# Eight-expert layer in a GNN and transformer kernel: the last expert's tile moved to the end, its output spread by one-hot products, and the next tile's scaling cut in three

## Chip, cores and metric

The kernel runs on one core of one Trainium2 chip. The metric is the device time of one execution in microseconds. Times of this program are shown as the median of its runs; the trace comes from one further execution under the profiler.

## The reference, cut to what matters

The program first runs a two-layer graph convolution and a 12-head causal attention over 625 tokens of 768 values. The change concerns what comes after: each token goes to one of eight experts, by the largest of eight gate values, and the output of that expert is added to the token.

```python
h2 = _ln(x, ln2_g, ln2_b).reshape(-1, d)
gate_logits = h2 @ Wg                       # 625 x 8
w, sel = jax.lax.top_k(gate_logits, K)      # K = 1
w = jax.nn.softmax(w)
combine = zeros.at[arange(n)[:, None], sel].add(w)
hid = relu(einsum('nd,edf->enf', h2, W1) + b1[:, None, :])   # W1: 8 x 768 x 3072
y = einsum('enf,efd->end', hid, W2) + b2[:, None, :]         # W2: 8 x 3072 x 768
return x + einsum('ne,end->nd', combine, y)
```

## The kernel before

**Engines and order.** One core; each engine has its own program, written by hand in its block (SP issues the weight loads, POOL the others, ACT, DVE and PE compute), and they meet through semaphores. Nothing is reordered: an engine does what stands next, and waits if it must.

**Tokens to tiles.** The 625 tokens stand in five groups of 125 (`C = 5`, `P = 125`). DVE works out for every token its expert, its rank in it and a row number `slot` (L1088 to L1154). A tile is 128 rows (`CAP`) of one expert. An expert with more than 128 tokens would get further tiles at the end of the list; `over[0]` is their number `n_over`. POOL scatters the normalised tokens `n2` to the DRAM tensor `hs_d` by `slot` (L515), and gathers the bias rows of `b2` into `x2` (L520). Tile 0 doesn't wait for the scatter: PE picks its tokens with one-hot matrices `oh0` (L1552).

**A tile** (function `tile` on each engine). The expert's weights are 18.9 MB of float32 in 16 chunks, 8 of W1 and 8 of W2, each 128 x 2304 (1152 KB). A chunk is loaded to one of four buffers `raw` (L417, L420), copied by ACT to a rounded `whi` (L557, from `split_hi`), and DVE writes the rest, raw minus whi, to `wlo` (L825, from `split_lo`). There are four `whi`/`wlo` pairs. A `raw` buffer is free for the chunk four later when its `wlo` is written. PE makes three products for each pair of operands (hi x hi, hi x lo, lo x hi): 18 matmuls of 384 columns for a chunk. In step k of a tile ACT does `split_hi` of chunk k+3 and then reads out PE's result of chunk k-1 to `hid` (L792); DVE does `split_lo` of chunk k+2. For W1, PE turns `hid` around (L1566), DVE adds the bias (L1179), ACT and DVE split it to `hTTh` and `hTTl` (L557, L823). The W2 products (L1593) collect in PSUM banks 4 and 5 and are copied to `ysb` by ACT and DVE at the start of the next tile (L785, L1175), and stored by POOL to `ys_d` (L530).

**The next tile's tokens.** POOL loads them to `hs` (L527). After W2 chunk 1, PE turns them to PSUM banks 6 and 7 (L1544). ACT scales them in six pieces to `hgf` (L767) and rounds them to `hgh` (L557), all in step `k == FCH + 2` (`FCH = 8`), after the `split_hi` of that step. DVE writes `hgl` in the same step (L1158, recorded at L825), and only then goes on to the `split_lo` of the next step.

**End.** Tiles 1 to 7 run in a loop (`Fori(1, E)`). Then comes a loop of four turns (`K_OVER`) over the further tiles, each skipped by an `If` when `s >= n_over` (PE: L1605 to L1608); in this execution all four were skipped on every engine. Then `ysb` is filled for the last time (L812, L1211), stored (L541), and POOL gathers each token's row of `ys_d` to `x2` in five indirect DMAs (L545). DVE adds `x2` times the gate weight to `base` (L1214), and SP stores the five parts of the output (L435).

## Time and profile before

| | us |
|---|---|
| three runs | 962.91, 964.02, 969.46 (median 964.02) |
| profiled execution, its own time | 963.17 |
| span of the profiled execution | 961.6 |
| mean granted TensorE clock | 0.968 of full speed |
| busy: PE, PEld, DVE, ACT, POOL | 867.0, 835.7, 709.2, 545.3, 90.9 |

PE is the matmul array, PEld its weight loads. Times in the profile count from the start of the span; the device time is 1.6 us longer than the span. The expert tiles fill the stretch from about 474 us to 937 us; what follows is the end described above.

### The profile page before, as it was taken

How to read it: one execution, taken by the hardware profiler on the slowest of the kernel's cores; microseconds unless marked ns; L12 is line 12 of the kernel's file. 1: busy time of each engine (PE TensorE's matmuls, PEld its weight loads, DVE VectorE, ACT ScalarE, POOL GpSimd, SP SyncE). 2: the span in 40 equal slices, each digit the busy share in tenths (PEclk: the TensorE clock that was granted, in tenths of full speed). 3: DMA queues.
4: the chain of work that ended last, by engine and by line, in shares of the span. 5: the costliest groups of instructions: out<-in, count | busy, mean ns of one | idle time of the engine just before them, and what ended most of it. 6: DMA issues, size and time to landing. Idle time of an engine off the chain costs nothing.

```text
span 961.6 us, 14800 instructions
## 1 busy us (share of the span) xinstructions
PE 867.0 (90%) x5410; PEld 835.7 (87%) x5410; DVE 709.2 (74%) x1076; ACT 545.3 (57%) x753; POOL 90.9 (9%) x92
## 2 busy tenths in 40 slices
PE   7999898989997888898878899999999999999990
PEld 7999898989996667798868899999999999899990
DVE  7996265773327999744666998898979889897962
ACT  4503232352226787624447587787868788686850
POOL 2000014220003100021630000000000000000002
PEclk9999799999999998999898999999999999999995
DMA  7020008255217500230698999999999999999935
GB/s 220 10 91 1 2 1 150 69 154 101 99 50 212 197 1 1 82 99 1 219 268 322 306 354 340 371 327 381 347 350 332 342 373 331 380 337 353 350 130 177
DMA packets 117094, 197.88 MB, mean 206 GB/s; under 512 B 34599, under 2 KB 83967, under 8 KB 117046
## 3 DMA queue, kind: packets, MB, share of 16 engines
q1 hardware_dynamic: 107796, 169.08, 53.2%
q0 software_dynamic: 7424, 26.09, 8.4%
q10 hardware_dynamic: 1826, 2.06, 0.8%
q8 instruction: 32, 0.52, 0.2%
q14 instruction: 16, 0.13, 0.0%
HBM read 179.29 MB, written 17.90 MB: 205 GB/s over the span
## 4 chain that ended last, share of the span: by engine, by line
PE 51%; DVE 19%; DMA 14%; issue 7%; ACT 7%; POOL 2%; SPq 0%; DVEq 0%; ACTq 0%; POOLq 0%
PE ps L1579 13%; PE ps L1236 11%; DMA raw<-in_L_ffn_W 11%; PE ps L1593 7%; PE ps L1412 7%; DVE wlo L825 6%; PE ps L1265 4%; PE ps L1566 2%; PE ps L1472 2%; DVE pTl L825 2%; ACT whi L557 2%; ACT hgf L767 2%; DVE pr L1025 1%; DMA hs_d<-n,slot 1%; DVE pr L1032 1%
## 5 line engine op out<-in xcount | busy, mean ns | idle before, releaser
L825 DVE TENSOR_TENSOR wlo<-raw,whi 128x2304 fp32r<-128x2304 f32 x137 | 349.9, 2570 | 20.3 <-ACT whi L557 20.1
L557 ACT ACTIVATE whi<-raw 128x2304 fp32r<-128x2304 f32 x139 | 295.3, 2130 | 107.1 <-DMA raw<-in_L_ffn_W 66.1
L1579 PE MATMUL ps<-whi,hgh 128*128 128x384 f32 x384 | 135.1, 352 | 3.9 <-DVE hgl L825 2.8
L1593 PE MATMUL ps<-whi,hTTh 128*128 128x384 f32 x384 | 131.7, 343 | 0.0
L1579 PE MATMUL ps<-whi,hgl 128*128 128x384 f32 x384 | 130.8, 341 | 0.0
L1579 PE MATMUL ps<-wlo,hgh 128*128 128x384 f32 x384 | 130.0, 339 | 0.0
L1593 PE MATMUL ps<-wlo,hTTh 128*128 128x384 f32 x384 | 129.8, 338 | 0.0
L1593 PE MATMUL ps<-whi,hTTl 128*128 128x384 f32 x384 | 129.6, 338 | 0.0
L1579 PEld LDWEIGHTS ps<-whi,hgh 128*128 128x128 f32 x384 | 73.6, 192 | 4.3 <-DVE hgl L825 2.9
L1579 PEld LDWEIGHTS ps<-wlo,hgh 128*128 128x128 f32 x384 | 73.8, 192 | 0.0
L1579 PEld LDWEIGHTS ps<-whi,hgl 128*128 128x128 f32 x384 | 73.2, 191 | 0.0
L1593 PEld LDWEIGHTS ps<-wlo,hTTh 128*128 128x128 f32 x384 | 72.2, 188 | 0.0
L1593 PEld LDWEIGHTS ps<-whi,hTTh 128*128 128x128 f32 x384 | 72.1, 188 | 0.0
L1593 PEld LDWEIGHTS ps<-whi,hTTl 128*128 128x128 f32 x384 | 72.1, 188 | 0.0
L1265 PE MATMUL ps<-ohd,ohs 125*125 125x314 bf16 x400 | 58.9, 307 | 7.5 <-DVE ohd L877 5.8
L1265 PEld LDWEIGHTS ps<-ohd,ohs 125*125 125x125 bf16 x400 | 54.9, 142 | 10.3 <-DVE ohd L877 8.3
L1566 PE MATMUL ps<-ident,hid 128*128 128x128 f32 x192 | 32.6, 278 | 23.5 <-ACT hid L792 23.5
L1566 PEld LDWEIGHTS ps<-ident,hid 128*128 128x128 f32 x192 | 23.8, 142 | 30.2 <-ACT hid L792 28.6
L823 DVE SCALAR_TENSOR_TENSOR hTTl<-bia,hTTh 128x384 fp32r<-128x384 f32 x64 | 35.4, 553 | 19.4 <-ACT hTTh L557 19.4
L1179 DVE TENSOR_TENSOR bia<-ps,b1T 128x384 f32<-128x384 f32 x64 | 35.6, 556 | 15.5 <-PE ps L1566 15.5
L557 ACT ACTIVATE qh<-ps 64x125 fp32r<-64x125 f32 (+1 forms) x66 | 20.4, 309 | 44.9 <-PE ps L1412 23.0
L1449 PE MATMUL ps<-ident,pr 125*125 125x125 f32 x168 | 32.1, 307 | 10.9 <-DVE pr L1032 7.7
(264 smaller groups left out, 1744.6 us busy)
## 6 DMA issues: line engine op xcount, KB each, us to landing
raw<-in_L_ffn_W SPq DMA_DIRECT2D x128, 1152.0 KB, 7.0
hs_d<-bc POOLq DMA_DIRECT2D x13, 384.0 KB, 6.4
raw<-in_L_gnn_W SPq DMA_DIRECT2D x4, 1152.0 KB, 5.6
ys_d<-ysb POOLq DMA_DIRECT2D x9, 384.0 KB, 5.9
hs<-hs_d POOLq DMA_DIRECT2D x8, 384.0 KB, 5.5
raw<-in_L_ffn_Wv SPq DMA_DIRECT2D x6, 384.0 KB, 5.2
raw<-in_L_ffn_Wq SPq DMA_DIRECT2D x6, 384.0 KB, 5.2
raw<-in_L_ffn_Wk SPq DMA_DIRECT2D x6, 384.0 KB, 5.3
```

The lines of the kernel that those rows point to most:

```text
L557: act.activation(out_, in_, func).then_inc(s, 1)
L767: act.activation(hgf[:, m, :], blocks(6, 128, DC, CAP)[:, m, :], ACT.Identity, scale=lnT[:, 2 * DC + m:2 * DC + m + 1], bias=lnT[:, 3 * DC ...
L823: dve.scalar_tensor_tensor(out_, in_, 0.0, hi_, ALU.max, ALU.subtract).then_inc(s, 1)
L825: dve.tensor_tensor(out_, in_, hi_, ALU.subtract).then_inc(s, 1)
L1179: dve.tensor_tensor(bia[:, k % 2, :, :], blocks(2 + k % 2, 128, JW, CAP), bcol.rearrange("p (j o) -> p j o", o=1).broadcast_to((128, JW, C ...
L1236: ins = mm(ps[0:P, bank + half, 0:HB], l, rr, start=m == 0 and i == 0, stop=m == DC - 1 and i == 2)
L1265: ins = mm(ps[0:P, m, 0:HALF], ohs[:, i % EU, m * P:(m + 1) * P], ohd[:, i % EU, :], start=i in BOUNDS, stop=i + 1 in BOUNDS)
L1412: ins = mm(ps[:, 2 * (m % 2) + half, 0:HALF], l, rr, start=c == 0 and i == 0, stop=c == DC - 1 and i == 2)
L1449: ins = nc.tensor.transpose(turned_part(u)[:, b, :], pr[:, u % PRS, b * P:(b + 1) * P], ident[0:P, 0:P])
L1566: ins = nc.tensor.transpose(blocks(2 + k % 2, 128, JW, CAP)[:, j, :], hid[0:CAP, k % 2, j * 128:(j + 1) * 128], ident[0:CAP, 0:CAP])
L1579: ins = mm(ps[0:CAP, k % 2, 0:FW], l, rr, start=m == 0 and j == 0, stop=m == DC - 1 and j == 2)
L1593: ins = mm(ps[0:CAP, 4 + half, 0:HB], l, rr, start=k == 0 and j == 0 and jj == 0, stop=k == FCH - 1 and j == JW - 1 and jj == 2)
```

## The change

**Order of the tiles.** The loop runs tiles 0 to 6, then come the further tiles (if any), then expert 7 as the last tile, written out once more on every engine. The row numbers are shifted to suit: further tiles start at number 7 and expert 7's rows go behind them.

**The last tile's output** no longer goes through DRAM. DVE marks each token that belongs to it in `oh0` again (five operations, during tile 0), PE turns these marks in the place where the other tiles turn the next tile's tokens, and ACT copies them to `ohl`. At the end ACT and DVE split the last tile's output to hi and lo in two halves, PE multiplies each token group's marks with them (four matmuls for a group), and DVE adds the product, read from PSUM, to `base`. POOL stores the output of the tile before, and gathers the five groups' rows from `ys_d`, while the last tile runs; DVE adds these to `base` after its last `split_lo`. The output is stored from `base`.

**Scaling of the next tile.** ACT's six pieces are done two at a time in the steps FCH+2, FCH+3 and FCH+4, each after the `split_hi` of its step; DVE's `hgl` moves to step FCH+5, behind its last `split_lo`.

```diff
+LAST_BANK = (0, 2, 6, 4, 0)
+TILE_STEPS = {FCH + 2: (0, 1), FCH + 3: (2, 3), FCH + 4: (4, 5)}
...
+                     ("ohl", [128, C, P], F32R)])
@@ SP
-            with sp.Fori(1, E) as t:
+            with sp.Fori(1, E - 1) as t:
                 weights(t, t)
...
-                    weights(e, s + E)
+                    weights(e, s + E - 1)
+            weights(E - 1, n_over + E - 1)
             for c in range(C):
                 sp.wait_ge(s_fin, c + 1)
                 for r0, r1 in PARTS:
-                    sp.dma_start(tok(out)[r0:r1, c, :], x2[r0:r1, c, :]).then_inc(s_out, 16)
+                    sp.dma_start(tok(out)[r0:r1, c, :], base[r0:r1, c, :]).then_inc(s_out, 16)
@@ POOL
-            for t in range(E + 1, TILES + 1):
+            for t in range(E, TILES + 1):
                 g.dma_start(ys_d[t * CAP:(t + 1) * CAP, :], bc[0][0:CAP, :]).then_inc(s_zero, 16)
...
-            with g.Fori(0, E) as t:
+            with g.Fori(0, E - 1) as t:
                 tile(t)
...
-            g.wait_ge(s_yev, 2 * (n_over + E) + 2)
-            g.dma_start(ys_d[bass.ds((n_over + E) * CAP, CAP), :], ysb[0:CAP, :]).then_inc(s_ylast, 16)
+            g.wait_ge(s_yev, 2 * (n_over + E - 1) + 2)
+            g.dma_start(ys_d[bass.ds((n_over + E - 1) * CAP, CAP), :], ysb[0:CAP, :]).then_inc(s_ylast, 16)
@@ ACT
-                    if k == FCH + 2:
-                        tile_in(t + 2, DC * t + 2 * DC)
+                    if last:
+                        if k == FCH + 2:
+                            a.wait_ge(s_ohT, 1)
+                            hi(ohl[:, :, :], blocks(6, 128, C, P), s_ohl)
+                        continue
+                    if k in TILE_STEPS:
+                        tile_part(t + 2, TILE_STEPS[k])
+                    if k == max(TILE_STEPS):
+                        tile_hi(DC * t + 2 * DC)
...
-            act.activation(ysb[0:CAP, 0:HB], ps[0:CAP, 4, 0:HB], ACT.Copy).then_inc(s_yev, 1)
+            tile(n_over + E - 1, last=True)
+            for half in range(2):
+                a.wait_ge(s_yhalf, half + 1)
+                hi(hg[0][:, 3 * half:3 * half + 3, :], blocks(4 + half, 128, 3, CAP), s_yh)
@@ DVE
-            step(dve.tensor_tensor(own, own, kk, ALU.add))
-            dve.tensor_copy(slot[:, :], own).then_inc(s_slot, 1)
+            step(dve.tensor_tensor(kk, kk, late, ALU.add))
+            step(dve.tensor_tensor(home, own, kk, ALU.add))
+            dve.tensor_copy(slot[:, :], home).then_inc(s_slot, 1)
...
             tile_in(1)
+            for c in range(C):
+                dve.tensor_scalar(oh0[:, c, :], iotac[:, :], float(CAP * (E - 1)), own[:, c:c + 1],
+                                  ALU.add, ALU.is_equal).then_inc(s_ohe, 1)
             split_lo(3, 0)
...
-                    if k == FCH + 2:
+                    if k == max(TILE_STEPS) + 1 and not last:
                         tile_in(t + 2)
...
+            tile(E - 1, n_over + E - 1, last=True)
+            d.wait_ge(s_base2, C)
             for c in range(C):
                 d.wait_ge(s_yg[c], 16)
-                dve.scalar_tensor_tensor(x2[:, c, :], x2[:, c, :], wtok[:, c:c + 1], base[:, c, :],
+                dve.scalar_tensor_tensor(base[:, c, :], x2[:, c, :], wtok[:, c:c + 1], base[:, c, :],
+                                         ALU.mult, ALU.add).then_inc(s_yin, 1)
+            for half in range(2):
+                d.wait_ge(s_yh, half + 1)
+                part = slice(3 * half, 3 * half + 3)
+                lo(hg[1][:, part, :], blocks(4 + half, 128, 3, CAP), hg[0][:, part, :], s_yl)
+            d.wait_ge(s_yin, C)
+            for c in range(C):
+                d.wait_ge(s_sel, c + 1)
+                bv = base[:, c, :].rearrange("p (a b) -> p a b", a=2)
+                dve.scalar_tensor_tensor(bv, wide(LAST_BANK[c], P), wtok[:, c:c + 1], bv,
                                          ALU.mult, ALU.add).then_inc(s_fin, 1)
@@ PE
-            with pe.Fori(1, E) as t:
+            with pe.Fori(1, E - 1) as t:
                 tile(t)
             pe.wait_ge(s_route, 1)
             n_over = pe.value_load(over[0:1, 0:1], min_val=0, max_val=K_OVER)
             with pe.Fori(0, K_OVER) as s:
                 with pe.If(s < n_over):
-                    tile(s + E)
+                    tile(s + E - 1)
+            tile(n_over + E - 1, last=True)
+            pe.wait_ge(s_ohl, 1)
+            def spread_y(c, half):
+                for i, t in enumerate(hg):
+                    ins = mm(ps[0:P, LAST_BANK[c] + half, 0:HB], ohl[:, c, :],
+                             t[:, 3 * half:3 * half + 3, :].rearrange("p a b -> p (a b)"), start=i == 0, stop=i == 1)
+                return ins
+            pe.wait_ge(s_yl, 1)
+            for c in range(C - 1):
+                spread_y(c, 0)
+            pe.wait_ge(s_yl, 2)
+            for c in range(C - 1):
+                spread_y(c, 1).then_inc(s_sel, 1)
+            pe.wait_ge(s_fin, 1)
+            spread_y(C - 1, 0)
+            spread_y(C - 1, 1).then_inc(s_sel, 1)
```

What stands on ACT in steps FCH+2 to FCH+4 of tile 0 before (names in brackets are semaphores; chunks_used is counted by PE, tile_turned says that the next tile's tokens are in PSUM):

```order
L557 ACTIVATE whi<-raw 128x2304 [waits raw_in1,chunks_used]
L767 ACTIVATE hgf<-ps,lnT 128x128 [waits tile_turned]
L767 ACTIVATE hgf<-ps,lnT 128x128 x5
L557 ACTIVATE hgh<-hgf 128x768 [waits tile_scaled]
L557 ACTIVATE whi<-raw 128x2304 [waits raw_in2,chunks_used]
L557 ACTIVATE whi<-raw 128x2304 [waits raw_in3,chunks_used]
```

and in the changed kernel, whose lines here are numbered eight higher:

```order
L565 ACTIVATE whi<-raw 128x2304 [waits raw_in1,chunks_used]
L775 ACTIVATE hgf<-ps,lnT 128x128 [waits tile_turned]
L775 ACTIVATE hgf<-ps,lnT 128x128
L565 ACTIVATE whi<-raw 128x2304 [waits raw_in2,chunks_used]
L775 ACTIVATE hgf<-ps,lnT 128x128 [waits tile_turned]
L775 ACTIVATE hgf<-ps,lnT 128x128
L565 ACTIVATE whi<-raw 128x2304 [waits raw_in3,chunks_used]
L775 ACTIVATE hgf<-ps,lnT 128x128 [waits tile_turned]
L775 ACTIVATE hgf<-ps,lnT 128x128
L565 ACTIVATE hgh<-hgf 128x768 [waits tile_scaled]
```

Two weight copies have moved ahead of four of the scaling pieces and of the rounding.

On DVE, the end of the program before:

```order
L825 TENSOR_TENSOR wlo<-raw,whi 128x2304
L1207 UNCONDITIONAL_BRANCH
L1205 REGISTER_ALU
L1205 COMPARE_AND_BRANCH
L1209 ISA
L1211 COPY ysb<-ps 128x384
L1214 SCALAR_TENSOR_TENSOR x<-x,wtok,base 125x768 x5
```

and in the changed kernel:

```order
L844 TENSOR_TENSOR wlo<-raw,whi 128x2304
L1241 SCALAR_TENSOR_TENSOR base<-x,wtok,base 125x768 x5
L844 TENSOR_TENSOR hgl<-ps,hgh 128x384 x2
L1251 SCALAR_TENSOR_TENSOR base<-ps,wtok,base 125x768 x5
```

The branches of the further tiles now stand ahead of the last tile instead of behind it, and five more additions follow the last weight chunk.

## Rows read from the trace of the kernel before

**Rows 1.** The chain that ended last: start us, us, what (x count)

```profile
515.90 3.17 PE ps L1593 x18
...
574.70 3.17 PE ps L1593 x18
...
720.95 4.69 PE ps L1579 x18
...
854.70 3.17 PE ps L1593 x18
...
893.46 3.15 PE ps L1579 x18
896.61 0.33 PE ps L1566 x3
...
910.84 3.17 PE ps L1593 x18
...
917.49 0.65 PE ps L1544 x6
918.15 19.02 PE ps L1593 x108
```

**Rows 2.** Timeline of ACT: start us, us, line, operation [idle before <-releaser]

```profile
863.43 2.19 ACT L767 ACTIVATE hgf<-ps,lnT 128x128 f32<-128x128 f32 x6
...
876.20 2.13 ACT L557 ACTIVATE whi<-raw 128x2304 fp32r<-128x2304 f32 x1 [2.43 <-DMA raw<-in_L_ffn_W]
```

**Rows 3.** Timeline of DVE, the same stretch

```profile
866.53 0.96 DVE L825 TENSOR_TENSOR hgl<-hgf,hgh 128x768 fp32r<-128x768 f32 x1 [2.23 <-ACT hgh L557]
867.41 9.96 DVE L825 TENSOR_TENSOR wlo<-raw,whi 128x2304 fp32r<-128x2304 f32 x4
```

**Rows 4.** Timeline of PE, the stretch just after

```profile
888.81 0.55 PE L1566 MATMUL ps<-ident,hid 128*128 128x128 f32 x3 [1.53 <-ACT hid L792]
```

**Rows 5.** Stretches: length, busy of PE PEld DVE ACT POOL, clock, DMA share, GB/s

```profile
845.00:861.00 16.00, 16.00 (x97) 15.87 (x97) 16.00 (x14) 13.30 (x14) 0.00 (x0) 1.00 0.98 341
...
869.00:873.00 4.00, 4.00 (x25) 4.00 (x24) 4.00 (x3) 2.92 (x2) 0.00 (x0) 1.00 0.66 208
...
873.00:887.00 14.00, 14.00 (x82) 13.96 (x80) 11.73 (x6) 8.29 (x6) 0.54 (x1) 1.00 1.06 375
```

**Rows 6.** The end: chain that ended last

```profile
937.19 0.57 DVE ysb L1211
...
938.43 3.98 DMA ys_d<-ysb
...
948.82 7.47 DMA x<-ys_d,slot
...
956.31 1.02 DVE x L1214
```

**Rows 7.** One line's operations (ns min/median/max): the branches on PE, loads on DVE

```profile
L1602 PEldq COMPARE_BRANCH  x7: 76/208/220, 597.8 to 933.9; - x7
...
L1606 PEldq COMPARE_BRANCH  x4: 83/221/252, 938.7 to 941.7; - x4
...
L1607 PEldq COMPARE_BRANCH  x4: 221/224/3625, 934.9 to 941.3; - x4
...
L1206 DVEq TENSOR_LOAD <-over x4: 297/314/330, 928.0 to 931.6; - x4
```

**Rows 8.** Stretches behind the last matmul (columns as in rows 5)

```profile
937.00:940.00 3.00, 0.15 (x1) 0.00 (x0) 0.56 (x1) 0.49 (x1) 0.54 (x1) 1.00 0.18 67
940.00:961.00 21.00, 0.00 (x0) 0.00 (x0) 5.09 (x5) 0.00 (x0) 6.09 (x5) 0.50 0.60 193
```

**Rows 9.** Gathers beside weight loads in tile 0: a stretch

```profile
484.00:504.00 20.00, 13.02 (x77) 12.31 (x76) 12.25 (x13) 9.05 (x10) 4.84 (x5) 0.98 1.04 258
```

**Rows 10.** The chain that ended last, in the same part

```profile
492.20 15.75 DMA raw<-in_L_ffn_W
```

**Rows 11.** Timeline of DVE before the scatter

```profile
462.52 0.17 DVE L1143 TENSOR_TENSOR rt<-rt 125x5 f32<-125x5 f32 x1
```

More of the change, by code:

```diff
@@ L212, in build @@
         rt, tp, iotac, oh0 = R1["rt"], R1["tp"], R1["iotac"], R1["oh0"]
+        ohl = R3["ohl"]
         hTT = (R3["hTTh"], R3["hTTl"])
@@ L316, in build @@
         s_yg = [sem(f"y_back{c}") for c in range(C)]
+        s_ohe, s_ohT, s_ohl, s_yhalf, s_yh, s_yl, s_sel, s_yin = (sem(n) for n in (
+            "last_expert_marked", "marks_turned", "marks_ready", "last_y_half", "last_y_hi", "last_y_lo", "last_y_spread",
+            "other_y_added"))
         s_yev, s_yst, s_ylast, s_zt, s_fin, s_out = (sem(n) for n in (
@@ L761, in _, with tile_part @@
             split_hi(2, 0)
-            def tile_in(n_in, n_a):
+            def tile_part(n_in, part):
                 a.wait_ge(s_hgT, n_in)
-                for m in range(DC):
+                for m in part:
                     act.activation(hgf[:, m, :], blocks(6, 128, DC, CAP)[:, m, :], ACT.Identity,
@@ L769, in tile_in, with tile_hi, tile @@
                                    bias=lnT[:, 3 * DC + m:3 * DC + m + 1]).then_inc(s_hga, 1)
+            def tile_hi(n_a):
                 a.wait_ge(s_hga, n_a)
                 hi(hg[0][:, :, :], hgf[:, :, :], s_hgh)
-            tile_in(1, DC)
+            tile_part(1, range(DC))
+            tile_hi(DC)
             split_hi(3, 0)
-            def tile(t, first):
+            def tile(t, first=False, last=False):
                 for k in range(SCH):
@@ L798, in tile @@
                         hi(hTT[0][:, JW * (k - 2):JW * (k - 1), :], bia[:, k % 2, :, :], s_hTh2, ACT.Relu)
-                    if k == FCH + 2:
-                        tile_in(t + 2, DC * t + 2 * DC)
-            tile(0, True)
-            with a.Fori(1, E) as t:
-                tile(t, False)
+                    if last:
[7 more added lines that the diff above has]
+                        tile_hi(DC * t + 2 * DC)
+            tile(0, first=True)
+            with a.Fori(1, E - 1) as t:
+                tile(t)
             a.wait_ge(s_route, 1)
@@ L1117, in _ @@
             kk = rt[:, 6, 16:16 + C]
+            late = rt[:, 6, 24:24 + C]
+            home = rt[:, 9, 0:C]
             tk = rt[:, 8, 0:E * K_OVER].rearrange("p (e k) -> p e k", k=K_OVER)
@@ L1162, in _, with tile @@
             tile_in(1)
+            for c in range(C):
+                dve.tensor_scalar(oh0[:, c, :], iotac[:, :], float(CAP * (E - 1)), own[:, c:c + 1],
+                                  ALU.add, ALU.is_equal).then_inc(s_ohe, 1)
             split_lo(3, 0)
-            def tile(e, t, first):
+            def tile(e, t, first=False, last=False):
                 for k in range(SCH):
@@ L1189, in tile @@
                            hTT[0][:, JW * (k - 2):JW * (k - 1), :], s_hTl2, relu=True)
-                    if k == FCH + 2:
+                    if k == max(TILE_STEPS) + 1 and not last:
                         tile_in(t + 2)
-            tile(0, 0, True)
+            tile(0, 0, first=True)
             d.wait_ge(s_base, C)
@@ L1199, in _ @@
                                          ALU.mult, ALU.add).then_inc(s_base2, 1)
-            with d.Fori(1, E) as t:
-                tile(t, t, False)
+            with d.Fori(1, E - 1) as t:
+                tile(t, t)
             d.wait_ge(s_route, 1)
@@ L1555, in _, with tile @@
             keep_busy(TURN_BUSY, onesb[:, :], onesb[:, :], 3)
-            def tile(t):
-                first = isinstance(t, int)
+            def tile(t, first=False, last=False):
                 pe.wait_ge(s_hgl, t + 1)
@@ L1594, in tile @@
                                          stop=k == FCH - 1 and j == JW - 1 and jj == 2)
-                    ins.then_inc(s_used, 1)
+                        if last and k == FCH - 1:
+                            ins.then_inc(s_yhalf, 1)
+                    if not last or k < FCH - 1:
+                        ins.then_inc(s_used, 1)
                     if k == 0:
                         turn_hid(FCH - 1)
-                    if k == 1:
+                    if k == 1 and last:
+                        pe.wait_ge(s_ohe, C)
+                        for c in range(C):
+                            ins = nc.tensor.transpose(blocks(6, 128, C, P)[:, c, :], oh0[:, c, :], ident[0:P, 0:P])
+                        ins.then_inc(s_ohT, 1)
+                    elif k == 1:
                         tile_in(s_hs, 16 * t + 16, t + 1)
-            tile(0)
-            with pe.Fori(1, E) as t:
+            tile(0, first=True)
+            with pe.Fori(1, E - 1) as t:
                 tile(t)
```

26 lines of the change are left out of this document (12 added, 14 removed).

## The prediction

> **What bounds the kernel now.** I read the chain that ended last first. It shows the same picture tile after tile from 574 us on: PE carries it, chunk by chunk, and hands it to ACT, DVE and a weight load only around the passage from one tile to the next. That chain gives a floor for a tile [rows 1]: W1 is 8 chunks of 3.15 us with 7 turnings of 0.33 us between them (27.5), W2 is two chunks of 3.17, the last turning of 0.33, the 0.65 of the next tile's tokens and 19.02 for the other six chunks (26.35), together 53.85 us. The starts of W2 lie 280.0 us apart over five tiles (574.70 to 854.70), so the passages 1-2 to 5-6 cost 280.0 - 5 x 53.85 = 10.75 us above the floor, 2.15 each. Passage 6-7 costs 56.14 - 53.85 = 2.3, passage 0-1 58.80 - 53.85 = 4.95.
>
> Second, the timelines of ACT, DVE and PE at one passage tell why. ACT does the six scalings in one piece from 863.43 to about 865.7 and the rounding behind them, and only then the next weight copy [rows 2]. DVE stands still 2.23 us for that, writes hgl in 0.96, and has then four chunks to split in one go [rows 3]. As a raw buffer comes free only when its wlo is written, the load that could have been issued at about 864.3 + 2.55 = 866.9 is issued at 867.41 + 2.5 = 870.0. The DMA queues run partly dry for it (208 GB/s from 869 to 873) and are then full at 375 GB/s without catching up [rows 5]. ACT waits 2.43 us for a load at 876.20 [rows 2], and some chunks later PE waits 1.53 us for the hid that ACT has behind such a copy [rows 4]. Once the stall was so long that the clock fell: 18 matmuls took 4.69 instead of 3.15 us at 720.95 [rows 1].
>
> Third, the end. From the end of the last matmul at 937.19 to the end of the span at 961.6 PE has no part in it: 24.4 us of read-out, store, five gathers and five additions [rows 6].
>
> **The end, new.** Let the last matmul end at 0. The first half of the output (9 of 18 matmuls, 0.175 us each from 3.15 / 18) is complete 1.6 us earlier, and its split on ACT and DVE, two operations like the read-out of 0.57 [rows 6], is hidden by the second half. From 0: PE spreads the first half for four groups, 8 x 0.175 = 1.4; beside it the second half is split, 2 x 0.57 = 1.15. The second half of group 0 is two matmuls, 0.35, with a handover of some 0.2 it is there at 1.95. Then DVE sets the pace, five additions of 1.02 [rows 6] (these had one operand less in PSUM; I take the same), to 7.05. The fifth group waits for a bank but needs only 0.7 of PE. The output store behind the last addition takes what it takes now, 961.6 - 957.33 = 4.27. Sum 11.3 instead of 24.4: **-13.1 us**. If the five stores, now 1.02 apart, queue up, it is a microsecond less; range -12 to -13.6.
>
> The five additions of gathered rows (5.1 us) lie behind DVE's last weight split, where DVE has nothing to do until the last tile ends; hidden unless the gathers are over 10 us late.
>
> **The passages.** With the scaling in three, each weight copy comes at its own time; the two scalings, about 0.73 us, fit in the time in which ACT waits for PE to release a buffer. DVE no longer waits, so the loads are issued 1.7 to 3.1 us earlier. The copies that waited for loads then wait for PE, as in the middle of a tile. hgl comes some 7 us later than now but still about 7 us ahead of the next tile's first matmul. Whether the queues can deliver is close: 18.9 + 0.4 + 0.4 = 19.7 MB for a tile at 375 GB/s are 52.5 us, against a floor of 53.85. So the stall can go, with hardly any reserve. I take five sixths of the 10.75: **-9.0**, range 0 to -10.75; a gain on the other side of the floor is excluded, and a loss of 1 us a tile (hgl's 0.96 before the next wlo) is the unlikely other end. At 0-1, DVE's five additions to base stand between the tiles and stay there, so I take **-1.5** of 4.95 (0 to -4). Passage 6-7 is counted next.
>
> **The further tiles' loop in mid-stream.** All engines now pass the four skipped turns between tiles 6 and 7, where they did it at the end, when only POOL mattered. On PE the sequencer left the tile loop at 933.9, while the array had work to 937.19, and its last branch began at 941.7 [rows 7]. One branch, the first skip, took 3.63 us; the others 0.22. So the array stands idle from 937.2 to 941.8, and with the tile's own waits some 4.9 us. In the last rows the clock was full up to 940 and half after it, some 3 us behind the last matmul [rows 8]; I take that it falls here too and costs what it cost once, 4.69 - 3.15 = 1.5 [rows 1]. The 2.3 of the old passage go. Net 4.9 + 1.5 - 2.3 = **+4.1**, range 0 to +8. DVE's loads of the skipped turns are 1.2 us apart (928.0 to 931.6) [rows 7], about 6 us in all, and SP has a like loop before it issues expert 7's first load; both begin before PE's does and are hidden by PE's gap. If PE's gap were not there, they would cost some 3 us instead.
>
> **The gathers beside the last tile.** Five times 384 KB is 1.92 MB, at 375 GB/s 5.1 us of DMA time that tile 7 has not spent till now. They are issued in its W1 part, where the queues moved 341 of 375 GB/s [rows 5], a reserve of 9% or 2.5 us in 27.5; the idle gap before also lets the loads get ahead. From below the cost is 0. The nearest row from above is tile 0: there scatter and gathers ran beside the loads, the total fell to 258 GB/s, PE was busy for 13.0 of 20 us [rows 9], and one load took 15.75 us [rows 10]. That is 7 us for more than twice these bytes. I take **+2**, range 0 to +7.
>
> **Small ones.** The slots need two more DVE steps in a chain of 0.17 us ones [rows 11], 0.35 on the way to the scatter. The five new marks fall in a place where DVE waits for ACT; 0 to 1. Together **+0.4**. The zeroed tile more is far ahead under the attention, and copying the turned marks replaces ACT's scaling in the last tile: nothing.
>
> **Sum**, against the profiled execution's own 963.17: -13.1 - 9.0 - 1.5 + 4.1 + 2.0 + 0.4 = -17.1, so 946.1. That execution lies 0.85 below the median of 964.02, so I predict **947**.
>
> **The rivals.**
> A. The weight loads are the true bound, and the passages stay as they are: they only wait for data at another place. For it: 375 GB/s without a break from 873 to 887, and 52.5 against 53.85. Against it: 208 GB/s just before, and 341 in mid-tile. Then 9.0 + 1.5 are missing: 957.5. 10%.
> B. The gathers hurt as in tile 0, 7 instead of 2: 952. For it rows 9 and 10; against it, tile 0 carried the scatter too, and its gather of bias rows reads only eight different rows. 10%.
> C. The loop costs PE next to nothing, because its first skip took 3.63 us only with the array running empty. Then 947 less about 5: 942. 8%.
> D. Slower. The eight far branches on PE (four skips, four turns) each fetch their target, and in mid-stream they do it against weight loads. At 3.63 each that is 29 us instead of the 5.2 of rows 7, giving 971; at one and a half times that, since loads more than doubled their time in tile 0, 43.5 and 985. It decides from about 26 us on top of the forecast, that is, branches of 3.9 us. For it: one skip did cost 3.63. Against it: the same skip cost 0.22 three times more, and the tile loop's own branch, as far, cost 0.2 seven times [rows 7]. 4%.
>
> The Trainium skill (Runtime: NRT & Kernel Launch, section Instruction fetch mechanics) says that a taken branch whose target is outside the current window of two pages has to fetch the page by DMA before the engine goes on. By that rule all far branches here pay, which is rival D; the trace bears it out for one branch of the eight and for none of the loop's.
>
> **How the numbers follow.** The forecast has 68%; its own range, from the terms above, is 940 to 953. A measurement of this kernel tells about 1% (9.6 us) from no change. Faster by more, that is below 954.4: nearly all of the forecast, B mostly, C, and a little of A: 84%. Within 1%: most of A, the edges of the others: 13%. Slower: most of D, 3%. The range 939 to 957 leaves out D, half of A and something at the lower end.
>
> **What would show it.** In the new profile: the last matmul of W2 to the end about 11 us with PE, DVE and the stores in it and no POOL; distances between starts of W2 of 54 to 54.5 instead of 56.0 for tiles 1 to 6; no wait of hgl for ACT and no dip at the passage; a hole of about 5 us in PE before tile 7 and half clock after it; small waits of ACT for weight loads in tile 7 behind the gathers. It is wrong if the distances stay at 56 (A), if the hole is far from 5 us (C, D), or if tile 7's W1 takes over 31 us (B).

## The result, and the profile after

The changed kernel takes 959.45 us (median of 13 runs, 954.62 to 963.68); the kernel before took 964.24 in the same session (13 runs). The ratio is 0.9941, with a 95% interval of 0.9918 to 0.9964: half a per cent faster, 5 us where 17 were forecast, and above the range of 939 to 957. The profiled execution took 956.24 us with a span of 954.7, mean granted clock 0.967; it lies 3.2 us below the median of the changed kernel's runs. So the miss is 12.5 us in the median (959.45 against 947) and 10.2 us in the profile, whose terms the table compares.

A table of the starts of W2 of each tile (the first matmuls of L1593 before, L1630 after) shows where the time went. The rows that begin a passage or a tile in the chain that ended last give the same numbers.

| us, one profiled execution each | before | after | difference | forecast |
|---|---|---|---|---|
| up to tile 0's W2 | 515.90 | 517.44 | +1.5 | +0.4 |
| tile 0 to tile 1 | 58.80 | 57.38 | -1.4 | -1.5 |
| tile 1 to tile 6, five distances | 280.00 | 269.99 | -10.0 | -9.0 |
| tile 6's W2 to the last matmul of tile 7 | 82.49 | 98.10 | +15.6 | +6.1 (4.1 and 2.0) |
| last matmul to the end of the span | 24.4 | 11.8 | -12.6 | -13.1 |
| span | 961.6 | 954.7 | -6.9 | -17.1 |

Four of the five lines came within 1.1 us. Nearly the whole miss of the profile is in one: the last 98 us of PE's work, 9.5 us over the forecast.

**What went as forecast.** The chain that ended last, of the kernel after (start us, us, what), a steady tile and then the end:

```profile
690.72 19.00 PE ps L1630 x108
709.72 6.26 PE ps L1616 x36
...
942.91 1.81 PE ps L1660 x10
...
944.81 2.87 DVE base L1251 x3
```

At 709.72, 36 matmuls of the next tile's W1 follow the last of W2 without any step on another engine between them; [rows 1] and [rows 4] had the hand-over there. The five distances are 54.0 us on average, against a floor of 53.85. Behind the last matmul stand 1.81 us of PE, the additions and the store.

ACT in the same passage (timeline: idle before and releaser in brackets):

```profile
693.99 2.14 ACT L565 ACTIVATE whi<-raw 128x2304 fp32r<-128x2304 f32 x1 [1.06 <-PE ps L1630]
696.03 0.79 ACT L775 ACTIVATE hgf<-ps,lnT 128x128 f32<-128x128 f32 x2
697.09 2.14 ACT L565 ACTIVATE whi<-raw 128x2304 fp32r<-128x2304 f32 x1 [0.26 <-PE ps L1630]
```

Two scalings (0.79 us) fit between two weight copies, and ACT still waits for PE afterwards; in [rows 2] six of them stood ahead of a copy. The stretches of that passage (length, busy of PE PEld DVE ACT POOL, clock, DMA share, GB/s), the first two 15 and 19 us behind tile 3's start of W2, as in [rows 5] behind tile 6's, and the third in W1 of tile 7:

```profile
698.00:702.00 4.00, 4.00 (x25) 4.00 (x24) 3.46 (x3) 3.97 (x5) 0.00 (x0) 1.00 1.07 376
702.00:716.00 14.00, 14.00 (x82) 13.97 (x82) 11.29 (x6) 10.11 (x7) 0.54 (x1) 1.00 1.07 376
...
886.00:906.00 20.00, 18.05 (x107) 16.99 (x105) 16.95 (x14) 11.67 (x12) 7.57 (x3) 1.00 0.99 265
```

The dent of 208 GB/s in [rows 5] is gone: 376 GB/s from the first microsecond on. That settles rival A, which wanted the loads to be the bound; they run at full rate and keep up, with next to no reserve.

**What did not.** The third row is tile 7's W1 beside the gathers. The queues are in use for 0.99 of the time and move 265 GB/s, where they moved 344 in the second half of tile 7's W1 before (896 to 911 us) and 341 in tile 6's [rows 5]:

```profile
896.00:911.00 15.00, 15.00 (x93) 14.84 (x92) 15.00 (x15) 12.50 (x14) 0.00 (x0) 1.00 0.99 344
```

PE's timeline of the kernel after, the operations that stood waiting between tile 6's last matmul and tile 7's W2:

```profile
878.10 0.68 PE L1616 MATMUL ps<-whi,hgh 128*128 128x384 f32 x1 [6.98 <-issue]
...
897.29 0.55 PE L1603 MATMUL ps<-ident,hid 128*128 128x128 f32 x3 [0.63 <-ACT hid L803]
...
902.07 0.55 PE L1603 MATMUL ps<-ident,hid 128*128 128x128 f32 x3 [1.08 <-ACT hid L803]
...
910.15 0.90 PE L1603 MATMUL ps<-ident,hid 128*128 128x128 f32 x3 [4.39 <-ACT hid L803]
```

and from the chain that ended last:

```profile
878.10 8.13 PE ps L1616 x36
...
893.13 14.39 DMA raw<-in_L_ffn_W
...
911.05 5.37 PE ps L1616 x18
```

Against the floor of 80.2 us (53.85, and 26.35 for the last W2) the 98.1 contain 17.9. They are nearly all in these rows: 6.98 of hole, 1.83 for the time at half clock behind it (8.13 instead of 2 x 3.15; the granted clock was 0.50 from 878 to 880 us), 6.10 of waits for hid, behind a weight load that took 14.39 us, and 2.79 for the two groups after the longest wait (5.37 instead of 3.15, 0.90 instead of 0.33, at a granted clock of 0.50 from 911 to 915 us). Sum 17.7. The hole and its clock are 8.8 where the prediction had 6.4, and the gathers' part 8.9 where it had 2.0. "<-issue" at the first row means that no other engine was waited for: PE's own sequencer, the part that takes the branches, was late. Its branches (PEldq; ns, min/median/max), and DVE's first split behind its own four skipped turns:

```profile
L1652 PEldq COMPARE_BRANCH  x4: 221/224/5524, 868.9 to 877.3; - x4
```

```profile
868.25 5.03 DVE L844 TENSOR_TENSOR wlo<-raw,whi 128x2304 fp32r<-128x2304 f32 x2 [4.16 <-issue]
```

Again one skip of four pays, now 5.52 us (3.63 in [rows 7]), and three cost 0.22. All six kernels below and here that keep the skips on PE in this place show it, with 5.46 to 5.92 us. Beside full queues (378 GB/s from 868 to 870 us) a transfer of 16 KB on an instruction queue, taken here for the page behind the branch, began 3.1 us after it; in the kernel before, with no loads under way, 1.0 us after it.

### The profile page after: what moved, and what is told of

Its sections match the earlier page's. It is cut to its first block, busy times and chain, and to the rows that moved or that the text cites. A ratio compares the mean times of both kernels' runs of the same rounds, so it can differ in the third digit from the quotient of the medians.

```text
span 954.7 us, 14785 instructions
## 1 busy us (share of the span) xinstructions
PE 874.0 (92%) x5429; PEld 843.1 (88%) x5429; DVE 714.1 (75%) x1089; ACT 544.7 (57%) x748; POOL 95.1 (10%) x91
## 4 chain that ended last, share of the span: by engine, by line
PE 63%; DVE 18%; DMA 7%; issue 5%; ACT 4%; POOL 1%; DVEq 1%; SPq 0%; ACTq 0%; POOLq 0%
PE ps L1630 16%; PE ps L1616 14%; PE ps L1273 12%; PE ps L1449 7%; DMA raw<-in_L_ffn_W 5%; DVE wlo L844 5%; PE ps L1302 4%; DVE pTl L844 2%; PE ps L1509 2%; PE ps L1603 2%; DVE pr L1044 2%; DMA hs_d<-n,slot 2%; DVE pr L1051 1%; ACT whi L565 1%; POOL hs_d L523 1%
## 5 line engine op out<-in xcount | busy, mean ns | idle before, releaser
L1630 PE MATMUL ps<-whi,hTTh 128*128 128x384 f32 x384 | 131.6, 343 | 0.0
L1630 PE MATMUL ps<-wlo,hTTh 128*128 128x384 f32 x384 | 129.8, 338 | 0.0
L1630 PE MATMUL ps<-whi,hTTl 128*128 128x384 f32 x384 | 129.7, 338 | 0.0
L1630 PEld LDWEIGHTS ps<-wlo,hTTh 128*128 128x128 f32 x384 | 72.2, 188 | 0.0
L1630 PEld LDWEIGHTS ps<-whi,hTTh 128*128 128x128 f32 x384 | 72.2, 188 | 0.0
L1630 PEld LDWEIGHTS ps<-whi,hTTl 128*128 128x128 f32 x384 | 72.1, 188 | 0.0
```

The lines of the kernel that those rows point to most:

```text
L1630: ins = mm(ps[0:CAP, 4 + half, 0:HB], l, rr, start=k == 0 and j == 0 and jj == 0, stop=k == FCH - 1 and j == JW - 1 and jj == 2)
```

## Experiments

Ten kernels were run. All times are medians, and each ratio is against runs of the kernel before that were made beside it; their median was 964.79 us for e1 to e4, 966.36 for e5 to e8 and 963.79 for e9 and e10, so kernels of different groups are compared by their ratios. The distances come from one profiled execution of each kernel, and how far they vary from one execution to the next was not measured. The traces of e4_three_only and e8_one_loop_split are of the slowest execution of each (959.52 and 947.11 us), in which tile 0's W2 began only at 525.5 and 523.9. The texts written ahead of the runs give the hole before tile 7 as 7.5 us; between PE's weight loads the trace shows 7.30, between matmuls, as above, 6.98. First all distances in one table; "tile 6 to 7" is from start of W2 to start of W2, "tail" from the last matmul of W2 to the end of the span.

| kernel | us | ratio (95%) | five distances | tile 6 to 7 | tail |
|---|---|---|---|---|---|
| before | 964.24 | 1 | 280.0 | 56.1 | 24.4 |
| after | 959.45 | 0.9941 (0.9918 to 0.9964) | 270.0 | 71.9 | 11.8 |
| e1_gate | 955.19 | 0.9898 (0.9861 to 0.9934) | 270.9 | 63.5 | 17.5 |
| e2_pe_plain | 957.10 | 0.9932 (0.9906 to 0.9958) | 271.0 | 69.9 | 11.9 |
| e3_rows_direct | 954.94 | 0.9906 (0.9874 to 0.9938) | 270.3 | 67.8 | 11.8 |
| e4_three_only | 952.92 | 0.9864 (0.9824 to 0.9904) | 269.6 | 54.2 | 24.1 |
| e5_last_alone | 967.78 | 1.0017 (0.9997 to 1.0038) | 281.5 | 69.0 | 11.8 |
| e6_no_skips | 950.14 | 0.9834 (0.9796 to 0.9873) | 269.6 | 66.1 | 11.9 |
| e7_later_split | 949.77 | 0.9827 (0.9788 to 0.9866) | 270.0 | 63.6 | 13.7 |
| e8_one_loop_split | 939.95 | 0.9701 (0.9670 to 0.9731) | 269.3 | 55.3 | 13.5 |
| e9_dve_plain | 956.76 | 0.9936 (0.9903 to 0.9970) | 269.4 | 68.5 | 12.1 |
| e10_three_adds_ahead | 940.47 | 0.9752 (0.9689 to 0.9815) | 270.5 | 55.6 | 12.6 |

### The two halves of the change apart

**e4_three_only**: the kernel before, with only its scaling cut in three.

```diff
-                    if k == FCH + 2:
-                        tile_in(t + 2, DC * t + 2 * DC)
+                    if k in TILE_STEPS:
+                        tile_part(t + 2, TILE_STEPS[k])
+                    if k == max(TILE_STEPS):
+                        tile_hi(DC * t + 2 * DC)
@@ DVE
-                    if k == FCH + 2:
+                    if k == max(TILE_STEPS) + 1:
```

> The kernel before with the scaling of the next tile in three steps and hgl at step FCH+5, nothing else of the change. Theory (this alone gave the passages' 10.0 + 1.4 us, and passage 6-7 gives its 2.3 too): distances between starts of W2 of about 53.9 us, span 947.5 to 949, time 949 to 951, faster than the whole change. Rival (the passages improved because the order of the tiles or the code changed): distances stay at 56, span 959 to 962.

Measured: 952.92 us, 1.9 over the expected range, 1.4% faster than before, and its interval lies below that of the whole change. Six distances from tile 1 to tile 7 are 53.75 to 54.27, as the theory said.

**e5_last_alone**: the change with the scaling in one step again.

```diff
-TILE_STEPS = {FCH + 2: (0, 1), FCH + 3: (2, 3), FCH + 4: (4, 5)}
+TILE_STEPS = {FCH + 2: (0, 1, 2, 3, 4, 5)}
@@ DVE
-                    if k == max(TILE_STEPS) + 1 and not last:
+                    if k == FCH + 2 and not last:
```

> The change without its other half: the last expert is run last and spread by products, but the next tile is scaled in one step at FCH + 2 again, on ACT and DVE. Theory (the two halves add up, and moving the last expert costs about as much before tile 7 as it saves behind it: 15.6 against 12.6 us): the five distances come back to 280 us in all, 10 us over those of the change, and the time is 966 to 971 us, not faster than before and likely 2 to 6 us slower. Rival (the last expert moved is a gain of some us by itself, and only hidden by the tighter schedule of the three parts, which leaves the loads no slack for the gathers): the distance from tile 6's to tile 7's start is under 68 us here, and the time 958 to 963 us.

Measured: 967.78 us, ratio 1.0017 with 1 in the interval. The five distances are back at 281.5, the tail stays at 11.8, tile 6 to 7 at 69.0. Moving the last expert alone is no gain: 12.6 us saved at the end, 12.9 (69.0 - 56.1) given back ahead of it. The theory expected 2 to 6 us slower and got 1.4; the two halves do not quite add up, since 0.9864 x 1.0017 = 0.988 and the whole change has 0.994. The missing 0.006 is 5.8 us, against some 0.005 of uncertainty from the three intervals, and the distances show where most of it would lie: with the scaling in three the move costs 71.9 - 54.2 = 17.7 us ahead of tile 7 instead of 12.9. Of these 4.8 us, 1.9 are no cost of the move: passage 6-7 still had its own stall before (56.1 against 54.2), and behind the hole that stall no longer counts. The other 2.9 (71.9 against 69.0) would be the rival's part, that the tighter schedule leaves the loads less slack for the gathers; one execution of each shows it. The whole gain of the change, and more, comes from the scaling in three (0.9864 alone, 0.9941 with the last expert moved).

### What the last tile pays for: the gathers

**e1_gate**: the five gathers wait until ACT has copied the turned marks, some 10 us into W2 of tile 7.

```diff
             g.wait_ge(s_base2, C)
+            g.wait_ge(s_ohl, 1)
```

> The changed kernel, but POOL's five gathers wait for the copied marks (ohl), which ACT writes right after its copy of weight chunk 13 of the last tile, when only the last two loads are under way. Theory (the gathers take the DMA engines from the weight loads of the last tile's W1; that cost 9.2 us of waits and half clock there): the waits of 1.1, 1.6 and 4.9 us in W1 of the last tile go, the distance from the start of W2 of tile 6 to that of tile 7 falls from 71.9 to about 63 us, the hole of 7.5 us before tile 7 stays, the gathers end some 22 us into a W2 of 26 and delay nothing: span about 945.5 us, time 947. Rival (the waits come from the loads that SP and DVE issued late behind the skipped turns, and from the half clock after the hole): W1 of the last tile still waits as long, span 953 to 956.

Measured: tile 6 to 7 in 63.5 us as against 71.9, and W1 of tile 7 without a wait. The 8.4 us that this takes away are the gathers' part. But the tail grew to 17.5, since the gathers came too late, and so the time of 955.19 is 8 us over the expected 947. DVE and PE at the end of this kernel (timelines):

```profile
938.62 1.02 DVE L1242 SCALAR_TENSOR_TENSOR base<-x,wtok,base 125x768 f32<-125x768 f32 x1 [1.37 <-DMA x<-ys_d,slot]
939.55 1.02 DVE L845 TENSOR_TENSOR hgl<-ps,hgh 128x384 fp32r<-128x384 f32 x2
```

```profile
940.25 0.65 PE L1661 MATMUL ps<-hgh,ohl 128*125 128x384 f32 x1 [4.28 <-DVE hgl L845]
```

The split of y, the last tile's output (hgl), stands behind the fifth gathered addition on DVE, and PE waits 4.28 us for it. That is queueing, not bandwidth: the additions are needed only at the very end.

**e3_rows_direct**: the same bytes, but each gather replaced by a plain load of 125 rows in a row, so that tokens do not get their own rows of y.

```diff
-                g.indirect_dma_start(out=x2[:, c, :], out_offset=None, in_=ys_d[:, :],
-                                     in_offset=bass.IndirectOffsetOnAxis(ap=slot1[:, c:c + 1], axis=0)
-                                     ).then_inc(s_yg[c], 16)
+                g.dma_start(x2[:, c, :], ys_d[CAP + c * P:CAP + (c + 1) * P, :]).then_inc(s_yg[c], 16)
```

> The changed kernel with the five indirect gathers replaced by five plain loads of the same size, 125 rows standing next to each other, issued by POOL at the same place; the tokens' rows are not picked, so that part of the computation is left out. Theory (the indirect gather is poor traffic: the queues moved 264 GB/s beside it instead of 375, and it costs the weight loads 11 us of DMA time for 5.1 us worth of bytes): with plain loads the total stays near 375 GB/s, the waits in W1 of the last tile fall from about 7 to 1 to 3 us, span 947 to 950. Rival (any 1.92 MB at that place cost as much): waits as before, span 953 to 956.

Measured: 954.94 us with a span of 952.7, so between the theory's span (947 to 950) and the rival's (953 to 956); tile 6 to 7 in 67.8 us, 4.1 less than after, and still 4.3 more than in e1_gate. The stretch of W1 that answers to after's 265 GB/s, and its two parts:

```profile
886.00:906.00 20.00, 18.09 (x101) 17.67 (x100) 13.38 (x12) 14.18 (x14) 0.79 (x2) 0.93 1.03 320
...
888.00:898.00 10.00, 10.00 (x62) 9.90 (x61) 7.77 (x8) 7.17 (x8) 0.00 (x0) 1.00 1.04 263
898.00:906.00 8.00, 6.09 (x31) 5.76 (x30) 5.61 (x5) 5.84 (x6) 0.00 (x0) 0.85 1.00 378
```

So about half of the gathers' 8.4 us stays when the same bytes come as plain loads, and half goes. The rate doesn't tell the two forms apart: 263 GB/s with plain loads under way, 265 with gathers. What differs is how long they are under way. The plain loads' packets fill the 10 us from 888 to 898, and behind them the queues are back at 378 GB/s; the gathers' packets are spread over all 20 us from 886 to 906. POOL issued the five plain loads within 2.7 us and the five gathers within 11.3. Whether the longer time comes from the gathers' form or from their slower issue, no run separates.

**e7_later_split**: gathers released by the turning of the marks on PE, and two gathered additions (`add_y`, with `EARLY = 2`) ahead of the split of y, three behind it.

```diff
+            g.wait_ge(s_ohT, 1)
@@ DVE
+            for c in range(EARLY):
+                add_y(c)
...
-            d.wait_ge(s_yin, C)
-            for c in range(C):
+            for c in range(C):
+                if c >= EARLY:
+                    add_y(c)
+                d.wait_ge(s_yin, c + 1)
                 d.wait_ge(s_sel, c + 1)
```

> The change with its gathers released by the marks' turning on PE (about 7 us into W2 of tile 7) and DVE's gathered additions split: two ahead of the split of y, three behind it, each just ahead of its token block's last addition. The skipped turns stay. Theory (the gathers cost by running beside the last loads, and cost nothing behind them if no split of y is queued behind them): distance to tile 7 63 to 64 us as with the wait for the marks, tail 12 to 13.5 us instead of 17.5, time 950 us (948 to 952). Rival (gathers 4 us earlier collide with the last load, or the row-wise transfers are simply too slow for the 20 us that are left): PE waits 2 us or more in the last passes of W2, or the tail stays over 15 us, and the time is 953 or more.

Measured: 949.77 us, tile 6 to 7 in 63.6, tail 13.7, no wait of PE in W2. The first gather began 8.2 us behind the start of W2, against 10.4 in e1_gate, so only 2.2 us earlier and not 4. The rest is as the theory said, the tail 0.2 over its range; the 2 us of tail over after's 11.8 are the three additions now on the path (3.0 us), less 1.3 by which the stores, now further apart, end sooner behind the last one (3.9 instead of 5.2).

### What the last tile pays for: the skipped turns

**e2_pe_plain**: the four skipped turns taken out on PE only, so that PE could run no further tile; **e9_dve_plain**: out on DVE only; **e6_no_skips**: out on all engines. For PE:

```diff
-            pe.wait_ge(s_route, 1)
-            n_over = pe.value_load(over[0:1, 0:1], min_val=0, max_val=K_OVER)
-            with pe.Fori(0, K_OVER) as s:
-                with pe.If(s < n_over):
-                    tile(s + E - 1)
-            tile(n_over + E - 1, last=True)
+            tile(E - 1, last=True)
```

> The changed kernel with the four skipped turns left out on PE alone; what PE thereby leaves out is the tiles of an expert with more than 128 tokens, of which this input has none. Theory (the hole is PE's first skip, 5.5 us, plus the other branches): the hole before tile 7 falls from 7.5 to under 1 us and the half clock after it goes, together 9 us less; the loads of the last tile then have less lead, so the gathers' waits grow by up to 4: span 945.5 to 950. Rival (DVE's own skipped turns, 5.9 us, keep chunk 0's wlo away and hold PE as long): the hole stays over 4 us, span 951 or more.

Measured: 957.10, a clear miss of what was expected (945.5 to 950). The hole of 7 us went, and the waits in W1 of tile 7 took its place:

```profile
881.27 0.55 PE L1603 MATMUL ps<-ident,hid 128*128 128x128 f32 x3 [2.92 <-ACT hid L803]
...
900.45 0.73 PE L1603 MATMUL ps<-ident,hid 128*128 128x128 f32 x3 [4.45 <-ACT hid L803]
...
914.77 0.47 PE L1603 MATMUL ps<-ident,hid 128*128 128x128 f32 x1 [5.59 <-ACT hid L803]
```

Together 13.0 us of waiting where after had 6.1 and its hole of 7.0: the sum stays. Part of the half clock now falls in tile 7's W2 (4.16 us for its first 18 matmuls), which the distance leaves out; from tile 6's W2 to the last matmul of tile 7 it is 97.2 us against 98.1. A reading that fits: while PE stood in its hole the loads ran ahead, and what they had in hand then was spent beside the gathers.

> The change with DVE's four skipped turns left out, on DVE alone (so DVE could run no further tiles); PE, ACT, SP and POOL keep theirs. It asks which engine's skipped turns were worth the 7 us between PE's alone left out (957.1) and all left out (950.1). Theory (DVE's 4.16 us of idle time ahead of its first split of tile 7 makes raw buffers free later, and so the loads late): the idle row of 4.16 us goes, the hole of 7.5 us on PE stays, the waits in W1 of tile 7 shrink by 3 to 4 us, and the time is 953 to 956 us. Rival (PE's hole covers DVE's, so that either alone gives nothing, and only both together pay): the distance from tile 6 to tile 7 stays within 1 us of 71.9 and the time at 957 to 961.

Measured: tile 6 to 7 in 68.5, 3.4 less than after, with PE's hole as it was; the time of 956.76 is 0.8 over the range, and its ratio of 0.9936 is not told from after's 0.9941. So the 3.4 us rest on one execution of each, and by the times the rival, that either engine's turns alone give nothing, is not excluded. DVE's idle row only shrank:

```profile
866.65 5.03 DVE L844 TENSOR_TENSOR wlo<-raw,whi 128x2304 fp32r<-128x2304 f32 x2 [3.13 <-ACT whi L565]
```

From 4.16 us behind its own turns to 3.13 behind ACT, which passes four of its own. Here one engine's skipped turns hid behind another's.

> The change with its K_OVER skipped turns left out on all engines (PE, ACT, DVE, SP, POOL), so what is left out is the running of further tiles, of which these inputs have none. Theory (the hole before tile 7 lies beside the gathers and loads, which are late in any case, so that taking it away only moves the waits into W1): tile 6's to tile 7's distance stays at 66 us or more, with gaps in W1 of tile 7, and the time is 953 to 958 us, within 3 of the run with PE's turns alone left out. Rival (it was DVE's and ACT's own skipped turns that made the splits late when PE's were out, and the loads have room): the distance falls to 58 to 62 us and the time to 945 to 950.

Measured: 950.14 us. Tile 6 to 7 in 66.1, as the theory said (66 or more); the time is 3 us under its range, at the edge of the rival's; in the profiled execution tile 0's W2 began at 514.7, some 3 us earlier than after. With all turns gone tile 6 to 7 still takes 12.3 us more than the floor, and behind the last wait come 1.9 us of half clock in W2:

```profile
886.16 18.92 DMA raw<-in_L_ffn_W
...
908.62 5.04 PE ps L1612 x18
```

One load took 18.92 us (in e2_pe_plain one took 19.52), and the first 18 matmuls of W2 took 5.04 instead of 3.17 (granted clock 0.50 from 907.7 to 912 us). To the last matmul of tile 7 it is 94.3 us from tile 6's W2: all turns out give 3.8 us by that measure, DVE's alone 3.4 (94.7).

### Both causes taken away

**e8_one_loop_split**: e7_later_split, and in place of the skipped turns one loop over tiles 1 to `n_over + E - 2`, whose expert comes from a table; all further tiles can still run. On DVE:

```diff
-            with d.Fori(1, E - 1) as t:
-                tile(t, t)
             d.wait_ge(s_route, 1)
             n_over = d.value_load(over[0:1, 0:1], min_val=0, max_val=K_OVER)
-            with d.Fori(0, K_OVER) as s:
-                e = d.value_load(over[0:1, bass.ds(s + 1, 1)], min_val=0, max_val=E - 1)
-                with d.If(s < n_over):
-                    tile(e, s + E - 1)
+            with d.Fori(1, n_over + E - 1) as t:
+                e = d.value_load(over[0:1, bass.ds(t + 1, 1)], min_val=0, max_val=E - 1)
+                tile(e, t)
             tile(E - 1, n_over + E - 1, last=True)
```

> The same as the later gathers with DVE's additions split, and in place of the skipped turns the seven tiles and the further ones run in one loop whose end is read from the table, so that there is no branch over a body: nothing of the computation is left out. Theory (with the gathers out of the way the hole is on the path: 7.5 us of gap and 1.8 to 2.7 of half clock): distance to tile 7 54 to 57 us and the time 941 to 945 us. Rival (the loads bound tile 7 in any case, since the hole gives them time to run ahead): the hole goes, waits of as much come into W1 and W2 of tile 7, distance 61 or more, and the time is 949 or more.

Measured: 939.95 us, 3.0% faster than before, a microsecond under the expected range. All that PE's timeline still shows as idle from tile 6's start of W2 to tile 7's:

```profile
883.55 0.55 PE L1600 MATMUL ps<-ident,hid 128*128 128x128 f32 x3 [0.42 <-ACT hid L799]
...
887.89 0.55 PE L1600 MATMUL ps<-ident,hid 128*128 128x128 f32 x3 [0.66 <-ACT hid L799]
```

**e10_three_adds_ahead**: the same with three gathered additions ahead of the split of y (`EARLY = 3`).

> The one loop with later gathers, with three of DVE's gathered additions ahead of the split of y and two behind it. Theory (the third gather has landed by the time PE ends tile 7, since DVE idles 5 us ahead of the split, and each addition behind it is 1 us on the path): the tail falls by about 1 us, from 13.5 to 12.5 us, and the median by the same, to 939 us. Rival (the third gather lands after PE's end and holds up the split of y): the tail is 14 us or more.

Measured: the tail is 12.6 instead of 13.5 as the theory said, and the third addition is over before ACT has its part:

```profile
924.01 1.02 DVE L1233 SCALAR_TENSOR_TENSOR base<-x,wtok,base 125x768 f32<-125x768 f32 x1 [1.21 <-DMA x<-ys_d,slot]
927.82 0.56 DVE L837 TENSOR_TENSOR hgl<-ps,hgh 128x384 fp32r<-128x384 f32 x1 [2.79 <-ACT hgh L561]
```

The median is 940.47, ratio 0.9752 (0.9689 to 0.9815), which the runs cannot tell from e8_one_loop_split.

### The four cases side by side

Distance from tile 6 to tile 7, floor 53.85; in brackets from tile 6's W2 to the last matmul of tile 7, floor 80.2:

| | gathers beside W1 | gathers in W2 |
|---|---|---|
| skipped turns before tile 7 | 71.9 (98.1), after | 63.6 (89.8), e7_later_split |
| none | 66.1 (94.3), e6_no_skips | 55.3 (81.5), e8_one_loop_split |

By the numbers in brackets, which take in the half clock that falls in W2 of e6_no_skips, the turns cost 8.3 us with the gathers out of the way and 3.8 beside them; the gathers cost 8.3 beside the turns and 12.8 without. They overlap by 4.5 us. That a standing PE lets the loads run ahead would explain it; these are four single executions, and the times put after and e6_no_skips further apart (ratios 0.9941 and 0.9834). In the right column DVE's additions are split as well, which these distances do not contain; in the lower row the turns are left out in e6_no_skips and folded into the tile loop in e8_one_loop_split.

## Why the prediction was wrong, point by point

- **The end, new: -13.1.** Right, -12.6. PE's spreading took 1.81 us, the additions 4.71 instead of 5.1, and the gathered additions were hidden. The stores behind the last addition took 5.2 us instead of 4.27, the microsecond that the range allowed for; the two errors partly cancel.
- **The passages: -9.0 and -1.5.** Right, -10.0 and -1.4; the reserve of 1.35 us a tile was enough for five distances of 54.0. e4_three_only shows it by itself.
- **Small ones: +0.4.** The front came 1.5 later; but over the kernels' profiled executions tile 0's W2 began anywhere from 514.7 to 525.5, so this one is not told from chance.
- **The further tiles' loop in mid-stream: +4.1.** The mechanism on PE was right: hole, one paying skip, half clock behind it. Its size was not: 8.8 of hole and half clock instead of 6.4, so +6.5. The prediction took over 3.63 us for the paying skip from a part of the trace with idle queues. In mid-stream it was 5.52 (5.46 to 5.92 in six kernels), and the step that should have warned was there: rival D multiplied the price by one and a half "since loads more than doubled their time in tile 0", and the forecast did not. It also put DVE's skipped turns at nothing, "hidden by PE's gap": with them out and PE's gap as it was, e9_dve_plain's distance is 3.4 us shorter, though its time is not told from after's.
- **The gathers beside the last tile: +2.0.** This is the step that failed: 8.9 us of waits and half clock. It divided bytes by the full rate (5.1) and took off a reserve of 2.5. That counts the gathers as if they used the queues as well as weight loads do. Beside them the queues moved 265 GB/s: over the 20 us of that window 5.3 MB instead of 7.5, and 1.92 of these were the gathers'. The weight loads so missed 7.5 - 3.4 = 4.1 MB, 11 us at 375 GB/s; less the reserve of 2.5 that is 8.5, near what was measured. e1_gate confirms the size by taking it away (8.4). e3_rows_direct shows that plain loads of the same bytes lower the rate as far (263 GB/s) but are gone in half the time, and leave about half of the cost. The nearest row from above, tile 0 with 258 GB/s and a load of 15.75 us [rows 9, 10], was the right one: tile 7 showed 265 and 14.39. The prediction set it aside because tile 0's traffic was more than twice the bytes; the rate (258 there, 265 here) was the number to carry over, not the 7 us. Its own sign of being wrong for this rival, tile 7's W1 over 31 us, came true: W1 ran from 878.10 to 916.75, 38.7 us.
- **"The idle gap before also lets the loads get ahead."** It fits e2_pe_plain, where the waits grew by as much as the hole had been, but it was used to lower the gathers' cost only. It works both ways: the turns cost less beside the gathers (3.8 instead of 8.3 us), and the gathers more once the turns are gone.
- **Rivals.** B (tile 7's W1 like tile 0) came true in mechanism, with 8.9 instead of 7. A, C and D fell: the distances are 54.0, the first skip pays, the others do not. D's price of half as much again per paying branch was right (5.52 / 3.63 = 1.5), its number of branches was not. The Trainium skill's rule (Runtime: NRT & Kernel Launch, section Instruction fetch mechanics), by which every taken branch out of the window of two pages fetches, holds here too for only one branch of the eight; the traces say nothing of why.
- **The range.** Its upper end of 957 came from B (952) and half of A. The two terms that failed had ends of +8 and +7; the runs gave 8.8 - 2.3 = +6.5 and +8.9. The second end was too short, and the range took the terms one at a time, as if only one could go wrong. They went wrong together. That both did so for one reason, queues full from 863 us on that hold up a page's transfer and a load alike, fits the traces, but no run shows it. The median lies 2.5 us above 957, and the profiled execution, at 956.24, just inside.

## What to carry to other kernels

Where a transfer is moved beside a saturated stream, price it by the total rate seen in a stretch of that mix and the bytes the stream then misses, not by its own bytes over the full rate; count how long it will be under way, since that is where the two forms of the same bytes differed; and place it where the stream ends, then look what stands behind its consumers on each engine. In this kernel a skip over a large body cost nothing where PE had nothing to do and a hole in mid-stream; one loop with an end read from a table does the same without it. Two edits at one place hide each other: take each away alone and both together before giving either a price.

## What the runs showed of the hardware that was not expected

- **Beside the gathers the weight loads' own packets took longer.** In W1 of tile 7 the queues were busy for 0.99 of the time in both cases, yet moved 265 GB/s with the gathers and 344 without them (896 to 911 us of the kernel before). The queues of those two stretches (packets, MB, share of the 16 engines' time), first after, where q1 has the weight loads and q0 the gathers, then before:

```profile
q1 hardware_dynamic: 1240, 3.35, 61.9%
q0 software_dynamic: 1118, 1.92, 36.1%
```

```profile
q1 hardware_dynamic: 1745, 5.16, 98.9%
```

In the time that their packets took, the weight loads moved 271 GB/s with the gathers beside them (3.35 MB in 61.9% of 20 us) and 348 without (5.16 MB in 98.9% of 15 us). Gathers with few weight loads beside them, in e7_later_split at the end, kept the queues only half busy:

```profile
916.00:934.00 18.00, 18.00 (x105) 18.00 (x104) 11.60 (x7) 6.27 (x5) 11.81 (x5) 1.00 0.53 171
```

- **The time that POOL needs to issue a gather goes with what DVE does.** POOL and DVE in the kernel after:

```profile
885.96 1.20 POOL L553 DMA_INDIRECT x<-ys_d,slot  x1 [0.30 <-issue]
887.46 3.23 POOL L553 DMA_INDIRECT x<-ys_d,slot  x1 [0.30 <-issue]
```

```profile
886.60 0.56 DVE L1207 TENSOR_TENSOR bia<-ps,b1T 128x384 f32<-128x384 f32 x1 [7.93 <-PE ps L1603]
887.08 2.55 DVE L844 TENSOR_TENSOR wlo<-raw,whi 128x2304 fp32r<-128x2304 f32 x1
```

Three gathers issued while DVE stood idle (the last of them for its first half) took 1.20 to 1.24 us each; the next two, beside splits of 2.55 us, took 3.23 and 3.18. In e7_later_split the four beside DVE's splits took 2.16 to 2.91 us; in e1_gate the last two, with DVE idle or at its additions, 1.20. No run was made to test it.
- **The first skip is dearer beside full queues.** 3.63 us with no loads under way, 5.46 to 5.92 in the six kernels that have it beside full ones; the transfer of 16 KB on an instruction queue began 3.1 instead of 1.0 us after the branch. Why only the first of four pays stays open.
